# Moving the FFN's TensorE pieces four slots ahead in a hand-written order of five engines

## The reference

```python
x = x + tanh(g_xattn) * xattn(layernorm(x), ctx, ctx, W, b, mask)   # softmax(q k / 4) v, then W, b
shared = swiglu(flat @ w_in.T) @ w_out.T          # 256 -> 2 x 512 -> 256
g_idx = argmax(flat @ wg.T + gb)                  # one of 2 groups
topv, topi = top_k(softmax(logits of the group) * g_prob, 2)   # 2 of its 4 experts
routed = sum_e (swiglu(flat @ w1.T) * w_se[:, e]) @ w2[e].T
x = x + tanh(g_ffn) * (shared + routed)           # flat = layernorm(x)
```

## Time and profile before

| | |
|---|---|
| median of 3 runs | 1115.81 us (1114.1 to 1115.92) |
| the profiled execution, time | 1116.76 us |
| the profiled execution, span | 1115.0 us |
| PE busy | 1066.6 us, 96% of the span |
| DVE, POOL, ACT busy | 835.2, 520.2, 472.6 us |
| chain that ended last | PE 84%, DVE 9%, issue 3%, ACT 2%, POOL 1% |

### The profile page before, as it was taken

The page is one execution under the profiler, slowest core; times in us unless marked ns, Lnnn a source line. Parts: engine busy times, 40 slices in busy tenths (PEclk is TensorE's granted clock), DMA queues, the critical chain, the costliest instruction groups (busy, mean ns, idle before and its releaser), DMA issues.

```text
span 1115.0 us, 22178 instructions
## 1 busy us (share of the span) xinstructions
PE 1066.6 (96%) x7283; PEld 897.8 (81%) x7283; DVE 835.2 (75%) x1859; ACT 472.6 (42%) x722; POOL 520.2 (47%) x617
## 2 busy tenths in 40 slices
PE   5779999999999999999999999999998999999997
PEld 3557888788788888888887778888887888888886
DVE  6677886987987888878868765466443788888886
ACT  4566656555565666566565432233221111111110
POOL 6434447456465465474483333000002566666564
PEclk9899999999999999999999999999999999999999
DMA  7888856666765767576465113787553555554451
GB/s 144 179 173 129 201 136 120 149 131 146 122 152 126 119 142 141 122 143 156 111 96 135 31 38 127 241 261 225 183 171 116 161 164 153 164 158 155 151 169 64
DMA packets 108130, 161.84 MB, mean 145 GB/s; under 512 B 29101, under 2 KB 72943, under 8 KB 108017
## 3 DMA queue, kind: packets, MB, share of 16 engines
q1 hardware_dynamic: 96244, 122.40, 47.2%
q0 software_dynamic: 11776, 38.03, 11.3%
HBM read 76.43 MB, written 52.12 MB: 115 GB/s over the span
## 4 chain that ended last, share of the span: by engine, by line
PE 84%; DVE 9%; issue 3%; ACT 2%; POOL 1%; DMA 0%; POOLq 0%; ACTq 0%; DVEq 0%
PE ps L781 16%; PE ps L726 13%; PE ps L828 13%; PE ps L743 7%; PE ps L830 6%; PE ps L648 4%; PE ps L636 4%; PE ps L679 3%; PE ps L813 3%; PE ps L601 3%; PE ps L657 2%; DVE mneg L1230 2%; PE ps L631 2%; PE ps L607 1%; PE ps L702 1%
## 5 line engine op out<-in xcount | busy, mean ns | idle before, releaser
L828 PE MATMUL ps<-regr,gh 128*128 x600 | 221.5, 407 | 0.1
L905 ACT ACTIVATE Pt<-ps,pbias 77x1024 f32<-77x1024 f32 x128 | 141.5, 1106 | 89.8 <-PE ps L636 86.3
L830 PE MATMUL ps<-regr,gl 128*128 x600 | 169.9, 283 | 0.0
L828 PEld LDWEIGHTS ps<-regr,gh 128*128 128x128 f32 x600 | 113.8, 190 | 23.8 <-issue 0.5
L995 ACT ACTIVATE gh<-ps 128x512 fp32r<-128x512 f32 x75 | 44.8, 599 | 204.8 <-PE ps L813 204.8
L1420 POOL TENSOR_TENSOR gl<-gf,gh 128x512 fp32r<-128x512 f32 x64 | 82.5, 1291 | 99.2 <-ACT gh L867 98.9
L1230 DVE TENSOR_REDUCE mneg<-ps 128x8 f32<-128x616 f32 x128 | 100.3, 792 | 22.6 <-PE ps L601 15.8
L830 PEld LDWEIGHTS ps<-regr,gl 128*128 128x128 f32 x600 | 114.0, 190 | 0.0
L726 PE MATMUL ps<-x2h,winh 128*128 128x512 f32 x256 | 108.1, 422 | 0.6 <-DVE OHR L1110 0.6
L726 PE MATMUL ps<-x2h,winl 128*128 128x512 f32 x256 | 101.0, 394 | 0.0
L726 PE MATMUL ps<-x2l,winh 128*128 128x512 f32 x256 | 100.8, 394 | 0.0
(11 more groups left out here) (208 smaller groups left out, 2655.2 us busy)
## 6 DMA issues: line engine op xcount, KB each, us to landing
regr<-regr SPq DMA_DIRECT2D x96, 256.0 KB, 5.9
y_dram<-Pt SPq DMA_DIRECT2D x64, 256.0 KB, 2.1
regf<-in_x SPq DMA_DIRECT2D x32, 256.0 KB, 2.9
x<-in_x SPq DMA_DIRECT2D x32, 256.0 KB, 4.3
y_dram<-res SPq DMA_DIRECT2D x32, 256.0 KB, 2.4
regr<-regr SPq DMA_DIRECT2D x96, 77.0 KB, 6.8
x_dram<-x2h SPq DMA_DIRECT2D x14, 512.0 KB, 3.0
x_dram<-x2l SPq DMA_DIRECT2D x14, 512.0 KB, 3.8
```

Of the source, the lines that this page charges most:

```text
L828: e.matmul(o, gh2[:, k % 3, fc, :], w2v[:, bass.ds(val, 1), fc, :, :].rearrange("p o h d -> p (o h) d"), start=fc == 0, stop=False, skip_g ...
L830: m = e.matmul(o[:, 0, :], gl2[:, k % 3, fc, :], w2v[:, bass.ds(val, 1), fc, 0, :].rearrange("p o d -> p (o d)"), start=False, stop=fc == ...
L905: e.activation(Pt[0:K, 4 * k:4 * k + 4, :].rearrange("k (n j) t -> k n (j t)", n=2), bank_of["sc", b, k][0:K, :, :], ACT.Exp, bias=pbias[: ...
```

## The change

One number in the condition that paces the FFN changes, from 9 to 5. Two pieces still stand in each odd slot, but each pair stands four slots earlier: pieces 0 and 1 of a chunk, in slot 11 of an odd step before, now stand in slot 7 of it. The routing's steps ride on the pieces, yet each routing starts when its logits are there, so in steps 7 to 34 every route step stays in its slot. Before the first and behind the last step the shift shows: four pieces more stand in steps 5 to 34, and four fewer in the tail behind step 34.

```diff
             if slot == 3 and i + 2 < NB:
                 order.append(("load_x", i + 2, 0))
-            while at["ffn"] < (12 * (i - 5) + slot - 9) // 2 * 2:
+            while at["ffn"] < (12 * (i - 5) + slot - 5) // 2 * 2:
                 ffn(1 if i < NB - 1 else 3)
             if i == NB + 2 and slot == 4:
                 held = None
```

## The result

The changed kernel takes 1124.8 us (median of 6 runs, 1123.76 to 1128.32) against 1115.74 for the kernel before (6 runs, 1114.1 to 1116.84): ratio 1.0093, 95% interval 1.008 to 1.0106. It is slower, as forecast, but by 9.1 us instead of 4.1, just inside the upper end of the range. The profiled execution took 1123.76 us, the lowest of its six, and its span is 1122.0 us: 7.0 more than before.

A forecast was written before the change was run, and what follows sets the result against it. TensorE, busy 96% of the span, was taken as the bound, so only waits could change: -1.55 + 3.6 + 0 + 2.4 + 1.5 + 0.6 - 2.45 = +4.1 us on 1115.8, giving 1119.9 us, range 1112.5 to 1125.

The forecast's parts named there:

- start: Start of phase one: pieces 0 to 3 fill waits, 2.8 us less a later att chain of 1.25: -1.55 us.
- middle: Steps 7 to 30: one more DVE product and POOL low part in odd steps make PE wait, +7.5 us in all.
- steps 31 to 34: End of phase one: one of two added DVE products in slot 7 passes 0.6 us on, bounds 0 and 2.
- tail without what follows: Last rank: carry comes earlier, 0.95 us won, and full TensorE clock behind it, 1.5 us: -2.45 us together.
- Kind 2: Six steps from 10 to 30: the product added in slot 7 before delays att and the scores, 0.6 us each, +3.6.
- POOL's and the port's terms: Added low part in slot 11: POOL's lateness 0.4 us a cycle, +2.4; SBUF blocking of DVE 0.25 a cycle, +1.5.
- Kind 3 to 0: From slot 7 of kind 3 steps on: DVE pauses of 0.54 and 0.18 us absorb the added product; charged nothing.
- The 1.5 us for the clock: Behind the last rank: with a wait below 1 us TensorE keeps its full clock, 1.5 us won.
- They fill the first wait: At the start: four pieces moved earlier fill PE's 0.72 us wait for an exponential at 81.07.
- neutral middle: Rival: a DVE pause in kind 1 absorbs the product, only start and tail remain, -4.0 us, 1111.8; chance 0.2.
- the one that cancels: Rival: kind 2 costs 3.6 us, POOL's and the port's terms nothing; sum +0.2, 1116.0 us; chance 0.2.
- POOL's lateness builds up: Rival: the whole low part passes to PE in kinds 2 and 3, 7.8 us instead of 2.4, 1125.3; chance 0.1.

The follow-up runs named there:

- e14: Changed kernel with two indirect DMAs of each of six routings behind POOL's small operations and the last routing's behind the last low part: 1138.81 us, ratio 1.0199.
- e7: Kernel before, with the last two indirect DMAs of each of the first six routings behind POOL's next small operations, chip 14: 1115.93 us, ratio 1.0002.
- e7b: Kernel before with the last two indirect DMAs of each of the first six routings behind POOL's small operations, run on chip 4: 1115.38 us, ratio 0.9923.
- e4: Kernel before, plus one DVE reduction of 512 elements in slot 7 of odd steps 7 to 29, nothing moved: 1127.55 us, ratio 1.0031.
- e3: Changed kernel, but POOL makes the first low part of a chunk with piece 9 instead of piece 5, for 14 chunks: 1122.89 us, ratio 0.9984.
- e1: Changed kernel up to step 28, pieces two slots ahead in steps 29 and 30, old order from step 31: 1124.15 us, ratio 0.9995.
- before_again: Plain copy of the kernel before, on chip 3: 1123.84 us, ratio 1.0001.
- after_third: Plain copy of the changed kernel, on chip 4: 1125.16 us, ratio 1.0013 to the kernel before on that chip.
- after_again: Plain copy of the changed kernel, on chip 3: 1124.82 us, ratio 1.0007 to the kernel before on that chip.
- e5: Changed kernel with the last routing's indirect DMAs on POOL behind the last low part instead of ahead of the last two: 1122.74 us, ratio 0.9992.

## Why the prediction was wrong in size

The terms in us, for the first pair of traces and for all traces of either order. In stretch 1 these are the means of nine of the old order and eight of the changed, without e14. In stretch 2 they are those without a pause of ScalarE, four of each; three of the old order have the two DMAs of kind 2 moved, which leaves it as it was. In the tail they are the six that keep the old order there. In brackets is what the term is with the lower clock of TensorE:

| term | forecast | first pair | all |
|---|---|---|---|
| start, stretch 1 less 2.8 | -1.55 | 92.0 - 90.2 - 2.8 = -1.0 | 92.6 - 89.75 - 2.8 = +0.1 |
| middle, stretch 2 | +7.5 | +6.45 | 456.6 - 450.1 = +6.5 |
| steps 31 to 34, stretch 3 | +0.6 | +3.4 | +2.0 (+3.4 if it is low in step 34 of the changed kernel) |
| tail without what follows | -2.45 | -2.6 | -2.2 (-2.7 if it is low behind the old order's rank, -1.2 if not) |
| index tile behind the tail | none | +1.45 | +1.4 |
| behind, and ahead of the first `att` | none | -0.7 | 0 |
| sum | +4.1 | +7.0 | +7.8 |

The medians are 9.1 us apart. The profiled execution of before was 1.0 us above its median and that of after 1.0 below, and e7's and e7b's, of the old order too, were 1.4 and 3.1 above theirs. So three of the traces without the pause are of slow executions of the old order, and a sum of traces comes out too small. Which stretch makes them slow is not known.

**What held.** The middle, by its mechanisms and nearly by its sizes. Kind 2 costs 0.54 us a cycle (forecast 0.6), and e4 shows its cause. The steps 12 to 28 take 4.5 us more (5 forecast). POOL's and the port's terms: kinds 3 and 0 cost 0.32 and 0.30 (0.4 and 0.25). Not all of kind 0 is the port's, though. Without the low part in slot 11 (e3) its wait for `mneg` is gone and kind 0 is at 19.45, 0.17 less; the wait of 0.25 for `att` stays. So some 0.13 us of kind 0 belong to "Kind 3 to 0", which the prediction put at nothing because of the pauses: they did not take in all of it. The fourth low part of the chunk ends at 269.01 and PE's piece 19 goes on at 269.07. Kind 1 costs nothing. The tail: the window behind the last rank is at 1.00 instead of 0.72, so no part of it at 1.2 GHz, and the rank waits 0.73 us instead of 1.79, 1.06 less (the prediction took 0.95, though its own times for `carry` give 0.83). PE's timeline:

```profile
678.80 0.18 PE L757 MATMUL ps<-OH,upb 128*128 128x48 bf16 x1 [0.73 <-DVE carry L1093]
```

The 1.5 us for the clock were in part luck. Of the six traces with the old order in the tail, four have 0.72 behind the rank (before, e1, e7, e7b; stretch 4 at 38.7 to 38.9 us). before_again and e4 waited 1.97 and 1.80 us and stayed at 1.00 (37.5 and 37.3). The changed order has 1.00 there in all of its traces.

**The step that failed most in the first pair: "Steps 31 to 34".** The term was mis-sized: 0.6 us for one product in a full queue, bounds 0 and 2, where the pair measured 3.4 and traces at full clock 2.0. I counted DVE's queue there and left POOL out. In step 32 the low part meets two small routing operations, 1.5 us in piece 7; e3 shows it. The rest of this pair's excess, 1.5 us, is TensorE's clock in step 34. The window has a mean of 0.86 above, with waits of 0.6 to 0.8 us in front; after_third has the same waits in the same order at full clock:

```profile
643.00:655.00 12.00, 10.66 (x68) 7.94 (x59) 11.41 (x36) 4.28 (x8) 2.52 (x2) 1.00 0.01 1
```

The loss belongs to one execution and not to the order (after_again doesn't have it either, before_again does).

**The start.** Over all traces this step failed as much: +0.1 instead of -1.55. "They fill the first wait" was wrong. Until the first piece the scores have three pairs of banks, and the third is the pair of the FFN:

```python
if ring == "P" and not turn["F"]:
    i = (0, 2, 6)[turn[ring] % 3]
```

The first piece takes a bank of it, whose last reader is ScalarE's exponential, so it waits itself (that the scores lose the third pair earlier may add to it; no run tried that). PE's timelines of the changed kernel, and of after_third with two of the matmuls that follow:

```profile
79.70 0.47 PE L726 MATMUL ps<-x2h,winh 128*128 128x512 f32 x1 [1.73 <-ACT Pt L905]
```

```profile
80.35 0.47 PE L726 MATMUL ps<-x2h,winh 128*128 128x512 f32 x1 [1.73 <-ACT Pt L905]
...
81.12 0.62 PE L726 MATMUL ps<-x2h,winh 128*128 128x512 f32 x1
81.53 0.63 PE L726 MATMUL ps<-x2l,winh 128*128 128x512 f32 x1
```

Before, PE waited 0.72 us in that place. Even so something is won up to the first `max` of step 6, which starts at 87.32 (88.2 forecast): from the `att` of batch 2 to it the changed kernel takes 22.1 us and the kernel before 20.3, 1.75 more for 2.8 us of pieces. Then, up to the `att` of batch 4, it gives back 1.3 us (18.1 against 16.8). Of these 0.9 are a meeting that the prediction did not list. In step 6 DVE makes the low part of a weight once (L1326, 1024 elements), and now POOL's L1490 (91.15 to 92.43), behind a new low part, and the L1474 that follows run beside it. DVE's and PE's timelines of before, then of the changed kernel:

```profile
90.64 1.21 DVE L1326 TENSOR_TENSOR wol<-res,woh 128x1024 fp32r<-128x1024 f32 x1
93.30 0.52 PE L601 MATMUL ps<-regr 128*128 128x308 f32 x2 [0.54 <-DVE mneg L1230]
```

```profile
91.38 2.13 DVE L1326 TENSOR_TENSOR wol<-res,woh 128x1024 fp32r<-128x1024 f32 x1
94.97 0.53 PE L601 MATMUL ps<-regr 128*128 128x308 f32 x2 [1.45 <-DVE mneg L1230]
```

The wait is 1.45 and 1.62 us in after_again and after_third too, 0.54 in before_again, and 1.13 in e3, where the low part is gone. That leaves +0.25 for the start. The -1.0 of the first pair comes from the clock in front of it: up to the `att` of batch 2 the kernel before took 33.3 us (0.80 from 33 to 50 us) and the changed one 32.0 (0.90). And in after_third the clock fell behind the first piece's wait (0.62 us a matmul instead of 0.40): the step around it took 21.57 us, where after_again, without that fall, took 20.42.
The Trainium skill, page "TensorE: Matmul & The Clock Gate", section "Part 1: The HAM clock gate (the "warmup" mystery)", ties the lower level to idle PE, and would have the clock stay up behind waits as short as these; in these traces it fell behind single waits of 1.73 us (after_third) and 1.79 us (before) in some executions, and behind the same waits in others it did not (after; before_again with 1.97).

**Behind the tail.** No term was there. I followed the rank and stopped. The low parts that the pieces need in the tail were moved behind the DMAs of the routing, in a queue that the prediction had itself called full (e5: 1.4 us).

The rivals: the neutral middle and the one that cancels are out. "POOL's lateness builds up" gave nearly the right number, 1125.3, for a wrong reason: kinds 2 to 3 cost 0.32, not 1.3. It did become real in e14.

## What to carry to other kernels

Where engines walk one order by hand, the price of moving a stage is the list of its new neighbours on every engine: two slots cost more than four. Sum each term up to the next point where all engines are idle, the tail's followers included, and ask of each wait to be filled whether the filler needs the same bank. Compare on more than one chip before a result of 1% is believed: here the chip moved the kernel before by 8 us and the changed one by none, and an edit of POOL's order that was worth nothing on one sort of chip was worth 0.8% on the other.

## What was unexpected of the hardware

- The same program takes 1115.6 or 1124 us by the chip, from a pause of ScalarE in each step of kind 2, beside two indirect DMAs of POOL: it is idle for 1.0 to 2.0 us, mostly 1.7, instead of 0.27. The pause is gone when the DMAs are issued some 4.5 us later (e7b). The profile puts it down to "remote". Its mechanism is open.
- A cast of 8 elements took 0.70 us instead of 0.17, and a three-operand operation of 64 elements 1.25 instead of 0.29, beside 512-element operations of POOL.
- An operation of 1024 elements took 2.13 us instead of 1.21 beside two of them.
- TensorE's granted clock fell in step 34 in some executions (0.86 over 12 us) and not in others of the same program, with waits of the same length; so it did behind the last rank of the old order, in four traces of six. Such a fall cost 1.2 to 1.5 us each time.
